# Moving the absolute sums of w_down from the context part into the attention steps

## The reference

```python
# x (16,100,512), ctx (16,361,512), 16 query heads, 4 key/value heads of 32
x = x + tanh(g_xattn) * attention(layernorm(x), ctx, mask, Wq, Wk, Wv, Wo)   # ALiBi, softmax over 361 keys
def weight_quant(w):                       # one scale for a whole matrix
    s = 1.0 / clip(mean(abs(w)), EPS)
    return clip(round(w * s), -1, 1) / s
h = silu(bit_linear(n, w_gate)) * bit_linear(n, w_up)      # n = layernorm(x), each 512 -> 2048
x = x + tanh(g_ffn) * bit_linear(rms_norm(h, ln_weight), w_down)     # 2048 -> 512
```

## Time and profile before

| | us |
|---|---|
| median of three runs | 536.34 |
| lowest and highest | 533.21, 541.49 |
| the profiled execution's own time | 538.78 |
| its span | 537.0 |
| PE busy (matmuls) | 478.4, 89% |
| DVE, ACT, POOL busy | 367.5, 329.6, 234.1 |
| mean granted clock of PE | 0.978 of full |
| chain that ended last | PE 56%, DMA 14%, DVE 11%, ACT 9% |
| DMA waits in that chain | ct<-ctx_t 7%, yq<-y_int 3%, qs<-nm_t 2%, wq_f<-wq 2% |

### The profile page before, as it was taken

The page is one execution under the profiler, slowest core; times in us unless marked ns, Lnnn a source line. Parts: engine busy times, 40 slices in busy tenths (PEclk is TensorE's granted clock), DMA queues, the critical chain, the costliest instruction groups (busy, mean ns, idle before and its releaser), DMA issues.

```text
span 537.0 us, 8363 instructions
## 1 busy us (share of the span) xinstructions
PE 478.4 (89%) x2887; PEld 301.7 (56%) x2902; DVE 367.5 (68%) x674; ACT 329.6 (61%) x560; POOL 234.1 (44%) x250
## 2 busy tenths in 40 slices
PE   2599979998989999997889999879899999999966
PEld 1599979997954444443444445435454555555522
DVE  4777634466555888885697785376777777777782
ACT  0366637565436656664756676577677777777760
POOL 1000000000146687855263670157666667677641
PEclk9999998999899999998999999999999999999988
DMA  7869897999748788879667721002533333333323
GB/s 189 266 186 406 331 354 279 236 345 289 150 88 201 176 184 203 192 153 237 147 136 172 159 96 73 29 0 39 119 79 79 78 78 78 78 74 77 75 52 68
DMA packets 55875, 83.94 MB, mean 156 GB/s; under 512 B 30787, under 2 KB 42259, under 8 KB 53919
## 3 DMA queue, kind: packets, MB, share of 16 engines
q1 hardware_dynamic: 50654, 58.30, 43.2%
q0 software_dynamic: 3456, 12.58, 8.7%
q10 hardware_dynamic: 1728, 12.58, 6.8%
HBM read 57.94 MB, written 9.85 MB: 126 GB/s over the span
## 4 chain that ended last, share of the span: by engine, by line
PE 56%; DMA 14%; DVE 11%; ACT 9%; issue 5%; POOL 2%; SPq 1%; ACTq 0%; POOLq 0%; DVEq 0%
DMA ct<-ctx_t 7%; PE bank L1335 6%; PE wide L1410 6%; PE bank L1325 6%; PE wide L1311 6%; PE bank L1420 6%; PE wide L1242 6%; PE bank L1242 6%; PE bank L1338 5%; PE bank L1283 5%; DMA yq<-y_int 3%; ACT p_t L709 3%; DVE row_max L982 3%; DMA qs<-nm_t 2%; DMA wq_f<-wq 2%
## 5 line engine op out<-in xcount | busy, mean ns | idle before, releaser
L982 DVE TENSOR_REDUCE row_max<-wide 100x2 f32<-100x722 f32 x128 | 110.4, 903 | 37.0 <-PE wide L1311 36.9
L709 ACT ACTIVATE p_t<-bank 121x400 f32<-121x400 f32 x192 | 92.4, 504 | 53.0 <-PE bank L1325 49.1
L1410 PE MATMUL wide<-w_q,xq 128*128 128x512 bf16 x372 | 86.6, 384 | 2.2 <-ACT xq L758 1.2
L565 POOL TENSOR_TENSOR z<-h,lnw 128x512 f32<-128x512 f32 x48 | 61.5, 1282 | 32.8 <-DVE h L1099 25.1
L1410 PEld LDWEIGHTS wide<-w_q,xq 128*128 128x128 bf16 x384 | 36.7, 99 | 48.6 <-issue 5.6
L1311 PE MATMUL wide<-ks,qs 101*100 101x362 f32 x192 | 50.0, 348 | 10.0 <-DVE row_max L982 5.2
L519 POOL DMA_DIRECT2D quant_in<-w_ffn x24 | 14.3, 597 | 101.4 <-PE bank L1283 94.9
L1325 PE MATMUL bank<-qs,ks 103*121 103x400 f32 x144 | 50.9, 385 | 6.5 <-DMA qs<-nm_t 2.9
L805 ACT ACTIVATE act<-wide,small 128x512 f32<-128x512 f32 x50 | 33.9, 679 | 32.6 <-PE wide L1410 21.6
L1283 PE MATMUL bank<-wv_f,ct 128*121 128x128 f32 x384 | 47.5, 283 | 3.7 <-DMA ct<-ctx_t 3.7
L1420 PE MATMUL bank<-w_q,yq 128*128 128x512 bf16 x189 | 46.9, 392 | 3.3 <-DMA yq<-y_int 2.7
(11 more groups left out here) (159 smaller groups left out, 936.1 us busy)
## 6 DMA issues: line engine op xcount, KB each, us to landing
quant_in<-w_ffn POOLq DMA_DIRECT2D x24, 512.0 KB, 6.1
ct<-ctx_t SPq DMA_DIRECT2D x16, 722.0 KB, 10.2
ks<-k_all SPq DMA_DIRECT2D x36, 181.0 KB
q_scratch<-qhl SPq DMA_DIRECT2D x16, 400.0 KB, 7.7
abs_a<-w_ffn ACTq DMA_DIRECT2D x6, 1024.0 KB, 7.4
abs_b<-w_ffn ACTq DMA_DIRECT2D x6, 1024.0 KB, 8.9
qs<-q_scratch SPq DMA_DIRECT2D x12, 400.0 KB
xb<-x SPq DMA_DIRECT2D x12, 256.0 KB, 2.7
```

Source lines behind the costliest of these rows:

```text
L565: nc.gpsimd.tensor_tensor(z[par][0:rows, c], h[0:rows, c], lnw[0:rows, c], ALU.mult).then_inc(z_done, 1)
L709: nc.scalar.activation(p_t[:, j, :], bank[j % 2][0:KT, 0:HQ], ACT.Exp).then_inc(exp_done, 1)
L982: nc.vector.tensor_reduce(row_max[b % 2][:, 2 * u:2 * u + 2], wide[u % 2][0:SQ, :, 0:SK], AX_X, ALU.max).then_inc(s_maxed, 1)
L1410: mm = nc.tensor.matmul(wide[j % 2][0:rows, m, :], xq[:, c, 0:rows], w_q[:, m * C + c, 512 * j:512 * j + 512], start=(c == 0), stop=(c == ...
```

## The change

The sums of w_gate and w_up stay where they were. Those of w_down leave the context part.

- `load_abs` and `sum_abs` stop at chunk 7 (`ABS_CTX`), so four loads of 1 MB and four additions fall away from context steps 4 to 12.
- ACT issues two loads (chunks 8 and 9) at the start of attention step 1, into two new buffers `abs_c`, once all K halves are made. They lie over the space of the context tiles, under the later `wo_f`. Chunks 10 and 11 are loaded when the four pieces of 8 and 9 are added.
- The additions are cut into 16 pieces of 128 x 512. `DOWN_AT` tells which pieces stand in which step: the first group of a step behind the exponentials of units 8 to 11, the second behind those of units 0 to 2. Steps 2 to 5 have three pieces each, steps 6 and 7 two each.
- In step 7 DVE adds the 16 sums behind the split of the maxima; in step 8, ahead of score group 3, PE adds over partitions and DVE makes the scale. SP's load of `wo` in step 8 waits for the 16 pieces, and POOL's half chunks 16 to 23 wait for the new scale.

```diff
-ABS_AT = {0: 5, 2: 6, 4: 7, 6: 8, 8: 9, 10: 10, 12: 11}
+ABS_CTX = 8
+ABS_AT = {0: 5, 2: 6, 4: 7}
+PIECES = 4
+DOWN_AT = {2: ((0, 1), (2,)), 3: ((3, 4), (5,)), 4: ((6, 7), (8,)), 5: ((9, 10), (11,)), 6: ((12,), (13,)), 7: ((14,), (15,))}
...
                 if b == 8:
+                    sp.wait_ge(down_piece, (WCH - ABS_CTX) * PIECES)
                     sp.dma_start(wo_f[:, :, :], wo).then_inc(wo_in, 16)
...
+            def load_down(n):
+                if n < 2:
+                    act.wait_ge(kl_ready, B)
+                else:
+                    act.wait_ge(down_piece, (n - 1) * PIECES)
+                act.dma_start(abs_c[n % 2][:, :], w_ffn[ABS_CTX + n]).then_inc(down_loaded[n % 2], 16)
+
+            def down_sums(pieces):
+                for i in pieces:
+                    n, k = divmod(i, PIECES)
+                    act.wait_ge(down_loaded[n % 2], 16 * (n // 2 + 1))
+                    c = abs_c[n % 2][:, k * F // PIECES:(k + 1) * F // PIECES]
+                    nc.scalar.activation(c, c, ACT.Abs, accum_out=down_abs[:, i:i + 1]).then_inc(down_piece, 1)
+                    if k == PIECES - 1 and n + 2 < WCH - ABS_CTX:
+                        load_down(n + 2)
...
             def attention_step(b):
+                if b == 1:
+                    load_down(0)
+                    load_down(1)
...
                     exps(b - 2, 8, 9, 10, 11)
+                if b in DOWN_AT:
+                    down_sums(DOWN_AT[b][0])
                 if b <= B:
                     exps(b - 1, 0, 1, 2)
+                if b in DOWN_AT:
+                    down_sums(DOWN_AT[b][1])
...
             def largest_scores(b, u):
                 dve.wait_ge(s_done, b * PAIRS + (u + 1))
+                if (b, u) == (8, 3):
+                    down_scales()
```

More of the change, by code:

```diff
@@ L183, in flamingo_block @@
     assert e <= r_i
+    abs_c, e = over(r_wo, ("abs_c0", [P, F], F32), ("abs_c1", [P, F], F32))
+    assert e <= r_i
     (oh, ol), e = over(r_wo, ("oh", [P, HPG, P], F32R), ("ol", [P, HPG, P], F32R))
@@ L215, in flamingo_block @@
     rstd = [cols(XG) for _ in range(2)]
-    w_abs = cols(WCH)
-    w_sum, w_mean, w_scale = cols(3), cols(3), cols(3)
+    w_abs, down_abs = cols(ABS_CTX), cols((WCH - ABS_CTX) * PIECES)
+    w_sum, w_mean, w_scale = cols(2), cols(2), cols(2)
+    down_sum, down_mean, down_scale = cols(1), cols(1), cols(1)
     f_bn, f_mv, f_ve, f_rstd = cols(6), cols(2), cols(1), cols(1)
@@ L271, in flamingo_block @@
         w_total = sem("w_total")
+        down_loaded = [sem(f"down_loaded{i}") for i in range(2)]
+        down_piece, down_stat, down_total = sem("down_piece"), sem("down_stat"), sem("down_total")
+        down_scale_set = sem("down_scale_set")
         w_scale_set = sem("w_scale_set")
@@ L523, in quantise @@
                 pool.wait_ge(quant_loaded[n % 2], (n // 2 + 1) * 16)
-                nc.gpsimd.tensor_scalar(buf, buf, w_scale[:, n // 8:n // 8 + 1], ROUND, ALU.mult, ALU.add).then_inc(quant_step, 1)
+                if n < ABS_CTX * 2:
+                    scale = w_scale[:, n // 8:n // 8 + 1]
+                else:
+                    pool.wait_ge(down_scale_set, 1)
+                    scale = down_scale
+                nc.gpsimd.tensor_scalar(buf, buf, scale, ROUND, ALU.mult, ALU.add).then_inc(quant_step, 1)
                 pool.wait_ge(quant_step, n * 2 + 1)
@@ L688, in ctx_step @@
             def ctx_step(b):
-                if ABS_EARLY < ABS_AT.get(b, WCH) + 1 < WCH:
+                if ABS_EARLY < ABS_AT.get(b, ABS_CTX) + 1 < ABS_CTX:
                     load_abs(ABS_AT[b] + 1)
@@ L963, in weight_sums, with down_sums, down_scales @@
             def weight_sums():
-                dve.wait_ge(abs_done, WCH)
-                nc.vector.tensor_reduce(w_sum, w_abs.rearrange("p (m c) -> p m c", m=3), AX_X, ALU.add).then_inc(wstat, 1)
+                dve.wait_ge(abs_done, ABS_CTX)
+                nc.vector.tensor_reduce(w_sum, w_abs.rearrange("p (m c) -> p m c", m=2), AX_X, ALU.add).then_inc(wstat, 1)
+            def down_sums():
+                dve.wait_ge(down_piece, (WCH - ABS_CTX) * PIECES)
+                nc.vector.tensor_reduce(down_sum, down_abs, AX_X, ALU.add).then_inc(down_stat, 1)
+            def down_scales():
+                dve.wait_ge(down_total, 1)
+                nc.vector.tensor_scalar(down_mean, wide[1][:, 1, 403:404], 1.0 / (D * F), Q_EPS, ALU.mult, ALU.max).then_inc(down_stat, 1)
+                dve.wait_ge(down_stat, 2)
+                nc.vector.reciprocal(down_scale, down_mean).then_inc(down_scale_set, 1)
+                dve.wait_ge(gate_done, 1)
+                nc.vector.tensor_scalar(w_dg, down_mean, gate_t[:, 1:2], 1.0 / 127.0, ALU.mult, ALU.mult).then_inc(down_stat, 1)
             def weight_scales():
                 dve.wait_ge(w_total, 1)
-                nc.vector.tensor_scalar(w_mean, wide[1][:, 1, 400:403], 1.0 / (D * F), Q_EPS, ALU.mult, ALU.max).then_inc(wstat, 1)
+                nc.vector.tensor_scalar(w_mean, wide[1][:, 1, 400:402], 1.0 / (D * F), Q_EPS, ALU.mult, ALU.max).then_inc(wstat, 1)
                 dve.wait_ge(wstat, 2)
@@ L1036, in _ @@
                 split_max(b)
+                if b == 7:
+                    down_sums()
                 if b == 10:
@@ L1296, in weight_totals, with down_totals @@
                 pe.wait_ge(s_maxed, 2 * PAIRS)
-                nc.tensor.matmul(wide[1][:, 1, 400:403], ones_all[:, :], w_sum, start=True, stop=True).then_inc(w_total, 1)
+                nc.tensor.matmul(wide[1][:, 1, 400:402], ones_all[:, :], w_sum, start=True, stop=True).then_inc(w_total, 1)
+            def down_totals():
+                pe.wait_ge(down_stat, 1)
+                nc.tensor.matmul(wide[1][:, 1, 403:404], ones_all[:, :], down_sum, start=True, stop=True).then_inc(down_total, 1)
             def scores(b, u):
@@ L1308, in scores @@
                     pe.wait_ge(nm_ready, b)
+                if (b, u) == (8, 3):
+                    down_totals()
                 for k in range(2):
```

2 lines of the change are left out of this document (removed).

## The result

| | before | after |
|---|---|---|
| median of 20 runs each, us | 537.99 | 542.19 |
| lowest and highest | 533.21, 544.14 | 539.61, 551.54 |
| the profiled execution, its span | 538.78, 537.0 | 542.40, 540.4 |
| mean granted clock | 0.978 | 0.972 |

The ratio after to before is 1.0103, 95% interval 1.0073 to 1.0134. Ratios leave out every run more than 1.5% above the fastest of its kernel, which is why this one lies above the 1.0078 of the two medians. So the change costs about 5.5 us, a loss clear of noise but under 2%. 534.9 us was predicted, with a range of 530.5 to 541.5. Of the 7.3 us between 534.9 and 542.19, 1.65 are the base (536.34 from three runs, 537.99 from twenty); the rest is the change.

What follows compares the result with a forecast made beforehand. The prediction took PE's idle places in the chain of waits as the bound, with the context tile `ct` weighing most. Its terms, -5.7 + 0.4 + 0.4 + 3.5 = -1.4 us, took the 536.34 us median to 534.9, range 530.5 to 541.5.

Steps and rivals of the forecast that it cites:

- Context part: Context steps 9 to 13: removing loads and additions ends PE's late-tile wait, step 9's loss and lower-clock loss, -5.7 us.
- ACT: Attention on ACT: pieces fit its idle times; load issues in steps 3 and 4 and at step 1 cost +0.4 us.
- Steps 7 and 8: Attention steps 7 and 8: PE's small matmul and DVE's three small instructions for the scale cost +0.4 us, between 0 and 1.0.
- DMA in attention: Attention steps 2 to 5: chunk loads delay the small store of maxima, +3.5 us, ends 0 and 12.4.
- the dearer end for the first pair: Upper cost of loading chunks 8 and 9 together at attention step 1, 3.6 us within the 12.4 end.
- four places that I priced: Holds of the store of maxima: 1.0 us in step 2, 0.3 in step 3, 0.9 in step 4, 1.3 in step 5.
- the second rival: Attention: store of maxima held up like behind wo, three places cost 12.4 us, so +7.5 and 543.8 us; chance 0.15.
- the dear end: Upper end of the DMA price in attention, 12.4 us: 4.4 for each of two later loads, 3.6 for the first pair.

Runs made afterwards that it cites:

- e1: Changed kernel without its four w_down chunk loads in attention, the 16 pieces adding other data; ratio to the kernel before 0.9897.
- e7: Changed kernel with chunks 8 to 11 loaded in context steps 4, 9, 12 and 15, none in attention; ratio to the kernel before 0.9892, median 532.64 us.
- e5: Kernel before with the 1 MB load of wo issued by ScalarE instead of SP in step 8; ratio to the kernel before 1.0017.
- e9: Second profile of the kernel before with wo's load issued by ScalarE instead of SP; this execution took 538.93 us.
- e2: Changed kernel with all four loads but each addition piece cut from 512 to 2 columns; ratio to the kernel before 1.015.
- e10: Changed kernel with each of the four loads cut to its first 1024 columns (512 KB); ratio to the kernel before 1.0046.
- e11: Changed kernel with each of the four loads cut to its first 32 rows (256 KB); ratio to the kernel before 0.997.

## Why the prediction was wrong

- **Context part, -5.7 us: right.** From step 12 to 13 the time fell from 9.61 to 5.93 us (3.7 of the 4.0 forecast), step 9 lost its 0.6 us, step 13 its 1.1 at the lower clock, and step 8 gave 0.4 more: 5.8. In this execution 1.1 was lost again in the step behind the hole of step 3, where the V matmuls took 5.48 us for 4.55, so the table shows 4.7. Without the chunk loads in attention (e1) and with them elsewhere (e7) the gain is there.
- **ACT, +0.4: nothing of it is shown.** Step 1 lost 0.64 where I had 0.2, but the same stretch took 13.92 us without any load (e1), and 12.35 (e5) and 13.94 (e9) in one and the same kernel: that is scatter. The pieces cost nothing (e1, e2), and the +0.1 for each issue in steps 3 and 4 isn't seen: there ACT waits for PE.
- **Steps 7 and 8, +0.4: right** (+0.5 in step 8, +0.14 in step 7). `wo`'s new wait and POOL cost nothing.
- **DMA in attention, +3.5: this is the step that failed.** It measured +10.0: step 2 5.8 for 1.0, step 3 0.2 for 0.3, step 4 4.2 for 0.9, step 5 -0.3 for 1.3. Two errors are in it. The first is the premise that ACT's loads would get the smaller share beside SP's. It came from one long load (12.3 us for chunk 11), which says nothing of a 6 KB store. In the trace the share was the other way round: until the store of step 2 was issued, the chunks had 66.5% of the engines and SP's queue 19.3%. So the Q and K rows ahead of the store were late, and it landed in 7.4 to 7.7 us where I had 3.0 and it had taken 1.8 before. The second is the dearer end for the first pair, 3.6 us, which was too low: behind the 3.74 us of idle time the clock was at 0.70 for 9.1 us, which I had priced in the context part and not here. Of the four places that I priced, two took nearly everything. In step 4 chunk 10 had landed (183.4) before the store was issued (184.3), and still the store took 5.3 to 6.2 us, behind the rows that the chunk had held up. In step 5 chunk 11, issued at 188.6, had landed (198.2) before the store at 200.2, and nothing was lost.
- **The mechanism was the second rival,** to which I gave 0.15: the two steps lost 5.8 and 4.2 us beside the 4.4 of `wo`'s step, 10 us in all against its 12.4. It would decide from 4.9 us on, as written, and did. Its size of +7.5 was 2 us above the measured 5.5. Its 543.8 us lay outside my own range, which ended at 541.5; the measured 542.19 lies between the two.
- **The rule that I cited against the change was right.** By the Trainium skill (DMA: Bandwidth & Descriptors, section Issuing engines are not separate DMA queues) a transfer on another engine's queue still runs on the same 16 engines. The trace agrees: 5.2 us for the store beside a load on ACT's queue (e9), and a ratio of 1.0017 for the move (e5). The row with 2.87 us of wait, in a step 4.4 us too long, was the nearest price, and I discounted it.
- **The working was asymmetric.** The DMA share of 0.87 and 5.7 us of spare for 12.2 us of work stood in the text. A mean share said that most of the work would not fit, and the forecast then took a quarter of the dear end.

## What to carry to other kernels

Moving a large load off a stretch where DMA engines are full only helps if nothing short and urgent runs where it goes: price it by the nearest small transfer with little slack, at the full price that a like load has anywhere in the trace, whichever engine issues it. Look also at what stands ahead of it in its own queue: here 1.17 MB of rows were just through when the store was issued, and any delay to them reached the store. If PE waits 3 us there, add what it then loses at the lower clock. Before moving work to another part, try to spread it within its own part, at places where the consumer waits least.

## What the runs showed of the hardware

- A 1 MB load issued by ACT also delays a 6 KB store issued by SP: 5.2 us to land in one execution (e9), 4.3 in another (e5), and 6.0 to 6.7 with `wo` on SP's queue (before), against 2.9 to 3.0 without such a load.
- Where two queues moved packets side by side, they moved about the same number, so the one with short packets got the smaller share of the time. In the changed kernel from 182.2 to 184.2 us, POOL's half chunk (4096 bytes a packet) moved 93 packets and 0.38 MB in 76.3% of the engines' time, SP's queue (K rows of 1448 bytes and a few shorter packets) 95 packets and 0.13 MB in 25.8%. In the kernel before (182 to 184 us) it was 75 and 72 packets.
- Two loads of 1 MB, issued together at about 147 us, landed after 6.0 and 11.7 us, two of 512 KB (e10) after 5.4 and 11.1, two of 256 KB (e11) after 3.5 and 6.4. The packets of all four loads took 10.2 us of 16 engines' time with half the bytes, against 13.9.
- One profile of a step that hangs on a small transfer is a draw, not a price: the same kernel's step 9 took 12.4 us in one execution and 15.0 in another, with a ratio of 1.0017 to the kernel before.
- Behind an idle time of 3.74 us the mean granted clock was 0.70 for the rest of the step (162.8 to 171.8 us) and behind one of 2.38 us 0.80 (191.1 to 199.6), a mix of 2.4 and 1.2 GHz; behind 0.36 us the V matmuls took 2.78 us as before it.
